# One selective-scan phase: the order of the read-backs, one GpSimd product per half step, and the remainder of the fp32r split made by TensorE

## The chip, the cores and the metric

The kernel runs on one NeuronCore of a Trainium2 chip. The metric is the device time of one execution in microseconds, the median of several runs. TensorE (PE in the profile), VectorE (DVE), ScalarE (ACT), GpSimd (POOL) and SyncE (SP, which here issues every DMA) each run their own instruction list in order and meet only at semaphores.

## The reference

The change lies in the first of two layers. For 8 images of 64 x 64 points with 192 inner channels, four directions k (rows, columns, and both reversed) each make

```
x_dbl = einsum('bkdl,kcd->bkcl', xs, x_proj_w)        # 6 rows for dt, 16 for B, 16 for C
delta = softplus(einsum(x_dbl[:6], dt_proj_w) + dt_proj_b)
h     = exp(delta * A) * h + (delta * u) * B          # 16 states for each channel, along 4096 points
y     = sum over states of h * C, + u * D
```

and the four y are added at their points. The rest (convolution before, normalisation and an output projection after, and a second layer with a Fourier resampling) is not touched.

## The kernel before

The program has three phases, one after another; the middle one, `scan_phase`, is changed. It walks 256 half steps, in the order image b (8), direction k (4), chunk ci of 1024 points (4), half of the channels (2). A half step m has 12 units: group g of four states (4) times block j of 32 channels (3). A unit is one tile of 128 partitions (32 channels x 4 states) by 1024 points. The two half steps of a chunk share the projected B and C. So 128 chunks, and within each an even and an odd half step.

**A unit.** ScalarE makes exp(delta A) (`exp`, line 735). For groups 0 to 2 TensorE spreads B over the partitions into a PSUM pair `P[un % 2]` (`fill`, line 553), VectorE multiplies it by delta u (`multiply`, 640), and scans (`scan`, 660). For group 3 GpSimd makes the product (`multiply`, 795) from a copy `brep`, ScalarE's exponential goes to `P[un % 2]`, and VectorE only scans. GpSimd then multiplies H by the spread C (`weigh`, 803), and TensorE sums the states into `yps` (`sum_y`, 589). Each engine's list is written out by unit number: TensorE does `fill(un + 1)`, ScalarE `exp(un + 1)`, VectorE `multiply(un)` and `scan(un)`, GpSimd `weigh(un - 1)`, and between them at fixed positions x = 0 to 11 of a half step the work for the next chunk. There are 4 buffers H, 3 buffers E (groups 0 to 2) and 7 buffers HC.

**The next chunk's work**, through one PSUM area `stage`, in this order: `project` (TensorE, fp32, line 537, x = 4 and 7 of the even half step, from `u`; for k = 1 and 3 it reads `u` by columns, one element in 64); two copies by ScalarE at x = 8, `dts` (693) and `sx` (694), the latter rounded to fp32r; the remainder `stage - sx` of rows 64 to 95 by VectorE (`split`, 625, after the scan of unit 8), so that the later spread in fp32r adds value and remainder; the delta matmuls (547) at x = 10 and in the odd half step at x = 4; three activations (702 to 706) at x = 11 and 5 that make softplus in `dlu`; VectorE's `delta` (634) that makes `dl`; GpSimd's product `dlu = dl * u` (`delta`, 788), both of them in the odd half step, at x = 1 and x = 7; and the spreads of C and B with their copies (553, 715, 719).

**SyncE** issues in one written order: for each half step the stores of `dl` and `dlu` to DRAM and their return as broadcasts `dlr` and `dur` (`spread_out`, `spread_in`, lines 468 to 485), the store of the finished y (`store_y`, 493), and for k = 2 and 3 the return of the y of the opposite direction into `yp` (`load_y`, 503), which TensorE adds at x = 5 (`sum_y`, line 583). `load_y(n + 1)` stands last in each half step n.

Of the kernel before, what the change touches and what calls it, by code (L numbers as in the profile page):

```python
# [7 lines left out]
ALU = mybir.AluOpType  # L8
# [8 lines left out]
C = 96  # L17
# [287 lines left out]
def scan_phase(nc, ctx, T, S):  # L305
# [13 lines left out]
    ds = T("ds", [C, 2, NK])  # L319
    dsum = T("dsum", [C, 2])  # L320
    idn = T("idn", [C, C])
    dg = T("dg", [C, 2, C])
    dlr = T("dlr", [128, 2 * NJ, TC])
    dur = T("dur", [128, 2 * NJ, TC])
# [30 lines left out]
    u_in = sem("u_in")  # L355
    x_done = sem("x_done")
    sx_copied = sem("sx_copied")
    sx_split = sem("sx_split")
    dt_done = sem("dt_done")
    softplus = sem("softplus_step")  # L360
# [49 lines left out]
    def slot(m, j):  # L410
        return j + NJ * (m % 2)

    def loaded(m):
        return 16 * (m // 2 + 1)
# [16 lines left out]
    def seconds(m):  # L431
        line, rest = divmod(m, NK * 2 * NCH)
        return line * 4 * NCH + max(0, rest - 4 * NCH)

    def rep_index(c, i):
        return 5 * c + i

# [13 lines left out]
    def sync(e):  # L451
        for t, n in consts:
            e.dma_start(t, S[n]).then_inc(consts_in, 16)

        def load_u(b):
            if b:
                e.wait_ge(x_done, 16 * b)
                e.wait_ge(dlu_made, 32 * b)
            for h in range(2):
                e.dma_start(u[:, h, :], S["xa"][b, h]).then_inc(u_in, 16)  # L460

        def spread_out(m):
            if m >= 2:
                for j in range(NJ):
                    e.wait_ge(dlr_in[slot(m, j)], loaded(m - 2))
                    e.wait_ge(dur_in[slot(m, j)], loaded(m - 2))
            e.wait_ge(dl_made, m + 1)
            e.dma_start(S["dl"][m % 2], dl).then_inc(dl_out, 16)
            e.wait_ge(dlu_made, m + 1)
            e.dma_start(S["dlu"][m % 2], dlu[:]).then_inc(dlu_out, 16)  # L470

        def spread_in(m):
            e.wait_ge(dlu_out, 16 * (m + 1))
            for j in range(NJ):
                if m >= 2:
                    e.wait_ge(mul_done, a_index(unit_of(m - 2, GB - 1, j)) + 1)
                    e.wait_ge(pool_mul_done, 3 * (m - 2) + j + 1)
                e.dma_start(dur[:, slot(m, j), :],
                            S["dlu"][m % 2, 32 * j:32 * j + 32, :].unsqueeze(1).to_broadcast([32, 4, TC])).then_inc(
                                dur_in[slot(m, j)], 16)  # L480
            e.wait_ge(dl_out, 16 * (m + 1))
            for j in range(NJ):
                if m >= 2:
                    e.wait_ge(exp_done, unit_of(m - 2, GB, j) + 1)
                e.dma_start(dlr[:, slot(m, j), :],
                            S["dl"][m % 2, 32 * j:32 * j + 32, :].unsqueeze(1).to_broadcast([32, 4, TC])).then_inc(
                                dlr_in[slot(m, j)], 16)

        def store_y(m):
            b, k, ci, half = steps[m]  # L490
            t0 = t_of(k, ci)
            e.wait_ge(y_copied, m + 1)
            e.dma_start(S["yk"][b, k % 2, half, :, t0:t0 + TC], yt[:]).then_inc(y_stored, 16)

        def load_y(m):
            if m == NSTEP or not second(m):
                return
            b, k, ci, half = steps[m]
            t0 = t_of(k, ci)
            e.wait_ge(y_stored, 16 * (steps.index((b, k - 2, NCH - 1 - ci, half)) + 1))  # L500
            if seconds(m):
                e.wait_ge(yp_added, seconds(m))
            e.dma_start(yp[:], S["yk"][b, k % 2, half, :, t0:t0 + TC]).then_inc(yp_in, 16)

        load_u(0)
        for m in range(2):
            spread_out(m)
            spread_in(m)
        for n in range(NSTEP):
            if n % 2 == 0:  # L510
                if n:
                    store_y(n - 1)
                if n + 2 < NSTEP:
                    spread_out(n + 2)
                    spread_in(n + 2)
            else:
                store_y(n - 1)
                if n + 2 < NSTEP:
                    spread_out(n + 2)
                if n % 32 == 29 and n + 3 < NSTEP:  # L520
                    load_u(n // 32 + 1)
                if n + 2 < NSTEP:
                    spread_in(n + 2)
            load_y(n + 1)
        store_y(NSTEP - 1)
        e.wait_ge(y_stored, 16 * NSTEP)

    def tensor(e):
        def project(c, sub):
            b, k, ci, _ = steps[2 * c]  # L530
            t0 = t_of(k, ci) + sub * 512
            if sub == 0:
                if ("x", c) in held:
                    e.wait_ge(*held["x", c])
                e.wait_ge(u_in, 32 * (b + 1))
            for h in range(2):
                r = e.matmul(stage[0:C + NR, sub * 512:(sub + 1) * 512], wx[:, k, h, :], view(k, h, t0, 512),  # L537
                             start=h == 0, stop=h == 1)
            if sub:
                r.then_inc(x_done)  # L540

        def delta(m):
            b, k, ci, half = steps[m]
# [48 lines left out]
                r.then_inc(y_summed)  # L592

        e.wait_ge(consts_in, NCONST)
        e.wait_ge(ve_set, 3)
        project(0, 0)
        project(0, 1)
        delta(0)
        delta(1)
        for i in range(5):  # L600
# [2 lines left out]
        for un in range(NUNIT + 12):  # L603
            n, x = divmod(un, 12)
            c = n // 2 + 1
            fill(un + 1)
            if un >= 5 and (un - 5) % 3 < 2 and (un - 5) // 3 < NG * NSTEP:
                sum_y((un - 5) // 3, (un - 5) % 3)
            if n % 2 == 0:
                if x < 3 and n and n < NSTEP:  # L610
                    rep(c - 1, x + 2)
                if x in (4, 7) and c < NCHUNK:
                    project(c, x // 7)
                if x == 10 and c < NCHUNK:
                    delta(n + 2)
            else:
                if x == 4 and c < NCHUNK:
                    delta(n + 2)
                if x in (8, 10) and c < NCHUNK:
                    rep(c, (x - 8) // 2)  # L620

    def vector(e):
        def split(c):
            e.wait_ge(sx_copied, c + 1)
            e.tensor_tensor(sx[64:96, c % 2, :], stage[64:96, :], sx[64:96, c % 2, :], ALU.subtract).then_inc(sx_split)  # L625

        def delta(m):
            b, k, ci, half = steps[m]
            kk = k * 2 + half
# [34 lines left out]
        e.tensor_copy(selb[:], selbf).then_inc(ve_set)  # L664
        e.memset(c20[:], 20.0).then_inc(ve_set)
        e.tensor_scalar(ndtb[:], dtb[:], -1.0, 20.0, ALU.mult, ALU.add).then_inc(ve_set)
        e.tensor_reduce(dsum[:], ds[:], AX.X, ALU.add).then_inc(skip_made)
        e.wait_ge(skip_made, 1)
        for half in range(2):
            e.tensor_scalar(dg[:, half, :], idn[:], dsum[:, half:half + 1], None, ALU.mult).then_inc(skip_made)  # L670
        split(0)
        delta(0)
        delta(1)
        for un in range(NUNIT):
            n, x = divmod(un, 12)
            c = n // 2 + 1
            if not on_pool(un):
                multiply(un)
            scan(un)
            if c < NCHUNK:  # L680
                if n % 2 == 0 and x == 8:
                    split(c)
                if n % 2 and x == 0:
                    delta(n + 1)
                if n % 2 and x == 6:
                    delta(n + 2)

    def scalar(e):
        def project(c):
            e.wait_ge(x_done, c + 1)  # L690
            if c >= 2:
                e.wait_ge(fill_done, 18 * (c - 1))
            e.copy(dts, stage[C:C + NR, :])
            e.copy(sx[:, c % 2, :], stage[0:C, :]).then_inc(sx_copied)

        def delta(m):
            b, k, ci, half = steps[m]
# [53 lines left out]
        e.activation(am[:], am[:], ACT.Exp).then_inc(a_made)  # L751
        e.wait_ge(a_made, 1)
        e.mul(am[:], am[:], -1.0).then_inc(a_made)
        e.wait_ge(ve_set, 3)
        project(0)
        delta(0)
        delta(1)
        for i in range(5):
# [3 lines left out]
        for un in range(NUNIT + 12):  # L762
# [5 lines left out]
            if n % 2 == 0:  # L768
                if 1 <= x <= 3 and n and n < NSTEP:
                    rep(c - 1, x + 1)  # L770
                if x == 8 and c < NCHUNK:
                    project(c)
                if x == 11 and c < NCHUNK:
                    delta(n + 2)
            else:
                if x == 5 and c < NCHUNK:
                    delta(n + 2)
                if x in (9, 11) and c < NCHUNK:
                    rep(c, (x - 9) // 2)
# [3 lines left out]
    def pool(e):  # L783
# [23 lines left out]
        for un in range(NUNIT + 1):  # L807
# [3 lines left out]
                weigh(un - 1)  # L811
            if n == NSTEP:
                break
            if x in (5, 7, 9):
                multiply(n, (x - 5) // 2)
            if c < NCHUNK and n % 2:
                if x == 1:
                    delta(n + 1)
                if x == 7:
                    delta(n + 2)  # L820

    run_block(nc, sync, tensor, vector, scalar, pool)

# [744 lines left out]
```

## Time and profile before

| | us |
|---|---|
| median of 3 runs (lowest, highest) | 13929.23 (13920.08, 13971.47) |
| the profiled execution: its time | 13937.71 |
| its span in the profile | 13935.9 |
| busy in the span: VectorE, TensorE, GpSimd, ScalarE | 12036.7, 10742.2, 10348.0, 6887.5 |
| mean granted clock of TensorE | 0.742 |

The span is cut by engine into busy and idle time; each idle stretch is put down to the instruction whose semaphore ended it. An instruction's line number names the place in the kernel. A timeline row gives start, duration, engine, line, operation, tiles and count; where neighbouring instructions are alike they are merged into one row with their number, and the bracket holds the engine's idle time before it and who ended it. An fp32 matmul counts as two matmuls in the profile and an fp32r one as one. The scan phase lies between 626 and 11274 us.

### The profile page before, as it was taken

The numbers are of one execution on the slowest core, as the hardware profiler recorded it, in microseconds if no ns is written. First come the engines' busy times: TensorE is split into PE (matmuls) and PEld (weight loads), VectorE is DVE, ScalarE is ACT, GpSimd is POOL, SyncE is SP. The second block draws the span as 40 slices with busy tenths as digits, with TensorE's granted clock in tenths as the row PEclk, the third lists the DMA queues.
The fourth block names the chain that finished last, engine by engine and source line by source line (L and its number), as shares of the span: only waits on it lengthen the run. The fifth ranks groups of instructions, "written<-read, shape, count | busy, mean of one in ns | idle before, by whom it ended". The sixth has DMA issues, their size and how long they took to land. (4 is left out here: it accounts for less than half of the span.)

```text
span 13935.9 us, 133740 instructions
## 1 busy us (share of the span) xinstructions
PE 10742.2 (77%) x41528; PEld 4591.2 (33%) x41528; DVE 12036.7 (86%) x8096; ACT 6887.5 (49%) x9171; POOL 10348.0 (74%) x4494
## 2 busy tenths in 40 slices
PE   8877777777777777777777777777777759999999
PEld 5522222222222222222222222222222237777778
DVE  7699999999999999999999999999999955555554
ACT  4355555555555555555555555555555533444443
POOL 1199889989998998999899999998899962222220
PEclk9866766666666666776677667766666768999999
DMA  3333332333333333333332333333333331111110
GB/s 105 112 102 113 113 122 101 105 118 120 108 105 109 124 108 111 118 104 111 116 121 101 110 115 124 103 103 113 123 111 107 109 90 37 41 40 37 37 37 10
DMA packets 371594, 1357.09 MB, mean 97 GB/s; under 512 B 47080, under 2 KB 47784, under 8 KB 367566
## 3 DMA queue, kind: packets, MB, share of 16 engines
q1 hardware_dynamic: 370894, 1348.53, 29.9%
q8 instruction: 344, 5.64, 0.2%
q14 instruction: 356, 2.92, 0.1%
HBM read 983.45 MB, written 364.90 MB: 97 GB/s over the span
## 5 line engine op out<-in xcount | busy, mean ns | idle before, releaser
L803 POOL TENSOR_TENSOR HC<-H,crep 128x1024 f32<-128x1024 f32 x3072 | 7227.9, 2365 | 989.9 <-DVE H L660 974.2
L553 PE MATMUL psum<-sx,selb 96*128 96x512 f32 x5888 | 3003.7, 610 | 2257.0 <-DVE H L660 1578.4
L660 DVE TENSOR_TENSOR_SCAN H<-E,car,psum 128x1024 f32<-128x1024 f32 x1728 | 4055.6, 2347 | 61.6
L553 PEld LDWEIGHTS psum<-sx,selb 96*128 96x128 f32 x5888 | 1296.9, 268 | 5496.1 <-issue 4553.1
L589 PE MATMUL psum<-HC,sely 128*32 128x512 f32 x12288 | 3080.9, 845 | 12.1 <-POOL HC L803 12.1
L640 DVE TENSOR_TENSOR psum<-dur,psum 128x1024 f32<-128x1024 f32 x2304 | 2784.0, 1208 | 230.4 <-PE psum L553 230.4
L735 ACT ACTIVATE E<-dlr,am 128x1024 f32<-128x1024 f32 x2304 | 2626.5, 1145 | 348.7 <-DVE H L660 347.3
L735 ACT ACTIVATE psum<-dlr,am 128x1024 f32<-128x1024 f32 x768 | 858.6, 1118 | 1971.5 <-DVE H L660 1963.3
L795 POOL TENSOR_TENSOR dbu<-dur,brep 128x1024 f32<-128x1024 f32 x768 | 1814.0, 2362 | 0.0
L741 ACT COPY car<-H 128x1 f32<-128x1 f32 x2304 | 425.7, 185 | 2117.8 <-DVE H L660 2111.1
L660 DVE TENSOR_TENSOR_SCAN H<-psum,car,dbu 128x1024 f32<-128x1024 f32 x576 | 1320.0, 2333 | 96.1 <-POOL dbu L795 93.1
L660 DVE TENSOR_TENSOR_SCAN H<-E,psum 128x1024 f32<-128x1024 f32 x576 | 1317.3, 2287 | 20.0
L547 PE MATMUL psum<-dlt,dtw 6*96 6x512 f32 x1024 | 822.8, 945 | 324.4 <-DVE sx L625 319.6
L1375 ACT ACTIVATE hs<-psum,b1a,co 128x512 f32<-128x512 f32 x768 | 555.7, 778 | 659.0 <-PE psum L41 658.6
L589 PEld LDWEIGHTS psum<-HC,sely 128*32 128x32 f32 x12288 | 376.2, 127 | 1490.1 <-issue 1305.2
L1409 POOL TENSOR_TENSOR y<-y,tmp 96x1024 f32<-96x1024 f32 x64 | 196.8, 3123 | 852.4 <-DMA tmp<-scr_yk 852.4
L537 PE MATMUL psum<-u,wx 96*102 96x512 f32 x1024 | 769.1, 885 | 30.5 <-DMA u<-scr_xa 30.5
L1155 PE MATMUL psum<-w2s,hs 128*128 128x96 f32 x6144 | 770.6, 284 | 0.6 <-DVE hs L1292 0.6
L788 POOL TENSOR_TENSOR dlu<-dlt,u 96x1024 f32<-96x1024 f32 x256 | 667.6, 2608 | 136.5 <-DVE dlt L634 136.5
L1155 PEld LDWEIGHTS psum<-w2s,hs 128*128 128x128 f32 x6144 | 731.6, 197 | 33.1 <-issue 5.3
L1292 DVE SCALAR_TENSOR_TENSOR hs<-psum,b1p,hs 128x512 f32<-128x512 f32 x768 | 544.2, 748 | 180.6 <-ACT hs L1375 180.4
L41 PE MATMUL psum<-xu,w1s 128*128 128x512 f32 x2304 | 603.1, 406 | 2.2 <-DVE xu L1279 2.2
(127 smaller groups left out, 10005.9 us busy)
## 6 DMA issues: line engine op xcount, KB each, us to landing
dur<-scr_dlu SPq DMA_DIRECT2D x768, 512.0 KB, 4.5
dlr<-scr_dl SPq DMA_DIRECT2D x768, 512.0 KB, 7.1
scr_dl<-dlt SPq DMA_DIRECT2D x256, 384.0 KB, 3.0
scr_dlu<-dlu SPq DMA_DIRECT2D x256, 384.0 KB, 3.0
scr_yk<-yt SPq DMA_DIRECT2D x256, 384.0 KB, 3.4
yp<-scr_yk SPq DMA_DIRECT2D x128, 384.0 KB, 8.9
scr_xa<-xs SPq DMA_DIRECT2D x64, 384.0 KB, 3.5
scr_sz<-xs SPq DMA_DIRECT2D x64, 384.0 KB, 3.5
```

Source lines behind the costliest of these rows:

```text
L41: r = e.matmul(o, w[p], x[q], start=first and i == 0, stop=last and i == 2)
L537: r = e.matmul(stage[0:C + NR, sub * 512:(sub + 1) * 512], wx[:, k, h, :], view(k, h, t0, 512), start=h == 0, stop=h == 1)
L547: r = e.matmul(stage[0:C, sub * 512:(sub + 1) * 512], dtw[C:C + NR, k * ND + half * C:k * ND + (half + 1) * C], dts[:, sub * 512:(sub + 1) ...
L553: r = e.matmul(o[:, sub * 512:(sub + 1) * 512], selb[:, which, :], sx[:, c % 2, sub * 512:(sub + 1) * 512], start=True, stop=True)
L589: r = e.matmul(yps[32 * j:32 * j + 32, cols], sely[:], HC[:, (3 * i + j) % NHC, cols], start=g == 0 and k == 1, stop=g == NG - 1)
L640: e.tensor_tensor(P[un % 2], dur[:, slot(m, j), :], P[un % 2], ALU.mult).then_inc(mul_done)
L660: e.tensor_tensor_scan(H[:, un % NH, ::step], decay[:, ::step], drive[:, ::step], init, ALU.mult, ALU.add).then_inc(scan_done)
L735: e.activation(o, dlr[:, slot(m, j), :], ACT.Exp, scale=am[:, ae:ae + 1]).then_inc(exp_done)
L788: e.tensor_tensor(shaped(dlu[:], k), shaped(dl, k), view(k, half, t_of(k, ci), TC), ALU.mult).then_inc(dlu_made)
L795: e.tensor_tensor(dbu[:, j, :], dur[:, slot(m, j), :], brep[:], ALU.mult).then_inc(pool_mul_done)
L803: e.tensor_tensor(HC[:, un % NHC, :], H[:, un % NH, :], crep[:, g, :], ALU.mult).then_inc(hc_done)
L1155: r = e.matmul(o[:, i * C:(i + 1) * C], hs[:, q % 2, j, i * 128:(i + 1) * 128], w2s[:, j, :], start=j == 0, stop=j == 2)
```

## The change

Three edits are made together.

1. SyncE's order: the stores and returns are split into four functions and regrouped. In an even half step n the `dlu` of n + 1 goes out and comes back, then y is stored and `load_y(n + 1)` follows. In an odd one `dl` and `dlu` of n + 1 go out and in, y is stored, `load_y(n + 1)` follows, and only then does SyncE wait for the `dl` of n + 2.
2. GpSimd makes `dlu` once in each half step, at x = 1 (`delta(n + 1)`; at the last half step of an image still one half step ahead, at x = 7), and its products for group 3 at x = 3, 5, 7 in place of 5, 7, 9.
3. The remainder: VectorE's `split` is gone. TensorE's new `rest(c)`, at x = 9 of the even half step, waits for the copy `sx`, repeats the projection into `stage` (fp32) and adds minus `sx` to it by a matmul in fp32r with `nid` (minus the identity, zero in rows 0 to 63). ScalarE's new `split(c)`, at x = 9 too, waits for that and copies rows 64 to 95 into `sx`. The delta matmuls wait for this copy, as they did for VectorE's.

```diff
         for n in range(NSTEP):
             if n % 2 == 0:
                 if n:
+                    if not ends_image(n + 1):
+                        out_dlu(n + 1)
+                        in_dur(n + 1)
                     store_y(n - 1)
+                load_y(n + 1)
+            else:
+                if n + 1 < NSTEP:
+                    out_dl(n + 1)
+                    out_dlu(n + 1)
+                    in_dur(n + 1)
+                    in_dlr(n + 1)
+                store_y(n - 1)
+                load_y(n + 1)
                 if n + 2 < NSTEP:
-                    spread_out(n + 2)
-                    spread_in(n + 2)
-            else:
-                store_y(n - 1)
-                if n + 2 < NSTEP:
-                    spread_out(n + 2)
-                if n % 32 == 29 and n + 3 < NSTEP:
-                    load_u(n // 32 + 1)
-                if n + 2 < NSTEP:
-                    spread_in(n + 2)
-            load_y(n + 1)
+                    out_dl(n + 2)
+                    if ends_image(n + 2):
+                        out_dlu(n + 2)
+                        if n + 3 < NSTEP:
+                            load_u(n // 32 + 1)
+                        in_dur(n + 2)
+                    in_dlr(n + 2)
...
+        def rest(c):
+            b, k, ci, _ = steps[2 * c]
+            t0 = t_of(k, ci)
+            e.wait_ge(sx_copied, c + 1)
+            for sub in range(2):
+                cols = slice(sub * 512, (sub + 1) * 512)
+                for h in range(2):
+                    e.matmul(stage[0:C, cols], wx[:, k, h, 0:C], view(k, h, t0 + sub * 512, 512), start=h == 0, stop=False)
+                r = e.matmul(stage[0:C, cols], nid[:], sx[:, c % 2, cols], start=False, stop=True)
+            r.then_inc(rest_done)
...
+                if x == 9 and c < NCHUNK:
+                    rest(c)
                 if x == 10 and c < NCHUNK:
                     delta(n + 2)
...
-                if n % 2 == 0 and x == 8:
-                    split(c)
...
+        def split(c):
+            e.wait_ge(rest_done, c + 1)
+            e.copy(sx[64:96, c % 2, :], stage[64:96, :]).then_inc(sx_split)
...
                 if x == 8 and c < NCHUNK:
                     project(c)
+                if x == 9 and c < NCHUNK:
+                    split(c)
                 if x == 11 and c < NCHUNK:
                     delta(n + 2)
...
-            if x in (5, 7, 9):
-                multiply(n, (x - 5) // 2)
-            if c < NCHUNK and n % 2:
-                if x == 1:
-                    delta(n + 1)
-                if x == 7:
-                    delta(n + 2)
+            if x == 1 and 2 <= n + 1 < NSTEP and not ends_image(n + 1):
+                delta(n + 1)
+            if x in (3, 5, 7):
+                multiply(n, (x - 3) // 2)
+            if x == 7 and n + 2 < NSTEP and ends_image(n + 2):
+                delta(n + 2)
```

## Rows read from the trace of the kernel before

**Rows 1.** Busy time of each engine over 10 ms of the scan phase (windows).

```profile
core 0: us, PE busy (x) PEld busy (x) DVE busy (x) ACT busy (x) POOL busy (x), PEclk, DMA share, GB/s
1000.00:11000.00 10000.00, 7348.71 (x19768) 2118.72 (x19769) 9580.05 (x5430) 5258.49 (x6880) 9076.49 (x3860) 0.69 0.33 112
```

**Rows 2.** The page's costliest groups: busy, mean ns, idle before with its releaser.

```profile
L803 POOL TENSOR_TENSOR HC<-H,crep 128x1024 f32<-128x1024 f32 x3072 | 7227.9, 2365 | 989.9 <-DVE H L660 974.2
...
L640 DVE TENSOR_TENSOR psum<-dur,psum 128x1024 f32<-128x1024 f32 x2304 | 2784.0, 1208 | 230.4 <-PE psum L553 230.4
...
L795 POOL TENSOR_TENSOR dbu<-dur,brep 128x1024 f32<-128x1024 f32 x768 | 1814.0, 2362 | 0.0
```

**Rows 3.** Who waited for GpSimd's products, line 795 (total us, times).

```profile
  DVE H L660: 131.1, 129
```

**Rows 4.** Timeline of VectorE at the end of an even half step.

```profile
5416.78 2.35 DVE L660 TENSOR_TENSOR_SCAN H<-E,car,psum 128x1024 f32<-128x1024 f32 x1
5419.16 1.22 DVE L625 TENSOR_TENSOR sx<-psum,sx 32x1024 fp32r<-32x1024 f32 x1
5420.41 6.83 DVE L660 TENSOR_TENSOR_SCAN H<-psum,car,dbu 128x1024 f32<-128x1024 f32 x3
5427.16 1.21 DVE L640 TENSOR_TENSOR psum<-dur,psum 128x1024 f32<-128x1024 f32 x1
```

**Rows 5.** Timeline of GpSimd near the end of an odd half step.

```profile
5046.17 2.84 POOL L788 TENSOR_TENSOR dlu<-dlt,u 96x1024 f32<-96x1024 f32 x1
...
5053.60 2.36 POOL L795 TENSOR_TENSOR dbu<-dur,brep 128x1024 f32<-128x1024 f32 x1
```

**Rows 6.** Timeline of VectorE in the same odd half step.

```profile
5055.99 2.29 DVE L660 TENSOR_TENSOR_SCAN H<-psum,dbu 128x1024 f32<-128x1024 f32 x1 [2.20 <-POOL dbu L795]
```

**Rows 7.** Timeline of SyncE's queue around a read-back of y.

```profile
5348.35 0.30 SPq L468 DMA_DIRECT2D scr_dl<-dlt  x1
...
5359.40 0.69 SPq L503 DMA_DIRECT2D yp<-scr_yk  x1
```

**Rows 8.** Timeline of TensorE at the use of that y.

```profile
5368.47 1.99 PE L583 MATMUL psum<-yp,idn 96*96 96x512 f32 x2 [3.71 <-DMA yp<-scr_yk]
...
5372.24 1.22 PE L553 MATMUL psum<-sx,selb 96*128 96x512 f32 x2
```

**Rows 9.** Timeline of VectorE at the same place.

```profile
5373.51 1.23 DVE L640 TENSOR_TENSOR psum<-dur,psum 128x1024 f32<-128x1024 f32 x1 [3.39 <-PE psum L553]
```

**Rows 10.** Timeline of ScalarE in the even half step of rows 4.

```profile
5416.97 1.00 ACT L693 COPY dlt<-psum 6x1024 f32<-6x1024 f32 x1
5417.98 1.01 ACT L694 CAST sx<-psum 96x1024 fp32r<-96x1024 f32 x1
5419.22 1.12 ACT L735 ACTIVATE psum<-dlr,am 128x1024 f32<-128x1024 f32 x1 [0.23 <-DVE H L660]
...
5422.85 1.12 ACT L735 ACTIVATE psum<-dlr,am 128x1024 f32<-128x1024 f32 x1 [2.40 <-DVE H L660]
```

**Rows 11.** Timeline of TensorE in that half step; the next chunk has k = 2.

```profile
5412.26 0.70 PE L553 MATMUL psum<-sx,selb 96*128 96x512 f32 x2 [0.95 <-DVE H L660]
5412.80 1.88 PE L537 MATMUL psum<-u,wx 96*102 96x512 f32 x4
5414.60 1.92 PE L589 MATMUL psum<-HC,sely 128*32 128x512 f32 x12
5420.43 3.72 PE L547 MATMUL psum<-dlt,dtw 6*96 6x512 f32 x4 [3.91 <-DVE sx L625]
```

**Rows 12.** Timeline of TensorE in another; the next chunk has k = 3.

```profile
2929.86 3.59 PE L537 MATMUL psum<-u,wx 96*102 96x512 f32 x4
2933.38 1.92 PE L589 MATMUL psum<-HC,sely 128*32 128x512 f32 x12
2937.49 1.95 PE L547 MATMUL psum<-dlt,dtw 6*96 6x512 f32 x4 [2.20 <-DVE sx L625]
2942.21 1.19 PE L553 MATMUL psum<-sx,selb 96*128 96x512 f32 x2 [2.76 <-DVE H L660]
```

**Rows 13.** Windows over the matmuls at 2929.86, 5412.80 and 5420.43; the clock is third from last.

```profile
2929.90:2933.40 3.50, 3.50 (x8) 0.52 (x6) 3.46 (x3) 0.63 (x1) 3.50 (x2) 1.00 0.00 0
5412.80:5414.70 1.90, 1.90 (x8) 0.60 (x9) 1.86 (x2) 0.00 (x0) 1.90 (x2) 1.00 0.03 9
5420.40:5424.20 3.80, 3.72 (x4) 0.95 (x4) 3.79 (x2) 1.40 (x4) 3.80 (x3) 0.50 0.00 0
```

More of the change, by code:

```diff
@@ L321, in scan_phase @@
     idn = T("idn", [C, C])
+    nid = T("nid", [C, C], F32R)
     dg = T("dg", [C, 2, C])
@@ L357, in scan_phase @@
     sx_copied = sem("sx_copied")
+    rest_done = sem("rest_done")
     sx_split = sem("sx_split")
@@ L433, in seconds, with ends_image @@
         return line * 4 * NCH + max(0, rest - 4 * NCH)
+    def ends_image(m):
+        return m % (NK * 2 * NCH) == NK * 2 * NCH - 1
     def rep_index(c, i):
@@ L460, in load_u, with out_dl @@
                 e.dma_start(u[:, h, :], S["xa"][b, h]).then_inc(u_in, 16)
-        def spread_out(m):
+        def out_dl(m):
             if m >= 2:
@@ L465, in spread_out, with out_dlu, in_dur @@
                     e.wait_ge(dlr_in[slot(m, j)], loaded(m - 2))
-                    e.wait_ge(dur_in[slot(m, j)], loaded(m - 2))
             e.wait_ge(dl_made, m + 1)
             e.dma_start(S["dl"][m % 2], dl).then_inc(dl_out, 16)
+        def out_dlu(m):
+            if m >= 2:
+                for j in range(NJ):
+                    e.wait_ge(dur_in[slot(m, j)], loaded(m - 2))
             e.wait_ge(dlu_made, m + 1)
             e.dma_start(S["dlu"][m % 2], dlu[:]).then_inc(dlu_out, 16)
-        def spread_in(m):
+        def in_dur(m):
             e.wait_ge(dlu_out, 16 * (m + 1))
@@ L480, in spread_in, with in_dlr @@
                                 dur_in[slot(m, j)], 16)
+        def in_dlr(m):
             e.wait_ge(dl_out, 16 * (m + 1))
@@ L506, in sync @@
         for m in range(2):
-            spread_out(m)
-            spread_in(m)
+            out_dl(m)
+            out_dlu(m)
+            in_dur(m)
+            in_dlr(m)
         for n in range(NSTEP):
@@ L594, in tensor @@
         e.wait_ge(consts_in, NCONST)
-        e.wait_ge(ve_set, 3)
+        e.wait_ge(ve_set, 4)
         project(0, 0)
         project(0, 1)
+        rest(0)
         delta(0)
@@ L622, in vector @@
     def vector(e):
-        def split(c):
-            e.wait_ge(sx_copied, c + 1)
-            e.tensor_tensor(sx[64:96, c % 2, :], stage[64:96, :], sx[64:96, c % 2, :], ALU.subtract).then_inc(sx_split)
         def delta(m):
@@ L666, in vector @@
         e.tensor_scalar(ndtb[:], dtb[:], -1.0, 20.0, ALU.mult, ALU.add).then_inc(ve_set)
+        e.tensor_scalar(nid[:, 0:64], idn[:, 0:64], 0.0, None, ALU.mult)
+        e.tensor_scalar(nid[:, 64:96], idn[:, 64:96], -1.0, None, ALU.mult).then_inc(ve_set)
         e.tensor_reduce(dsum[:], ds[:], AX.X, ALU.add).then_inc(skip_made)
@@ L670, in vector @@
             e.tensor_scalar(dg[:, half, :], idn[:], dsum[:, half:half + 1], None, ALU.mult).then_inc(skip_made)
-        split(0)
         delta(0)
@@ L753, in scalar @@
         e.mul(am[:], am[:], -1.0).then_inc(a_made)
-        e.wait_ge(ve_set, 3)
+        e.wait_ge(ve_set, 4)
         project(0)
+        split(0)
         delta(0)
```

## The prediction

> **What bounds the kernel now.** I read the busy time in windows first. Over 10 ms of the scan phase VectorE is busy 9580 of 10000 us, GpSimd 9076, TensorE 7349 and ScalarE 5258 [rows 1]: VectorE sets the pace, and only what leaves its list or ends a wait of its own is worth time. Next I read what VectorE waits for. Its products wait 230.4 us for TensorE's fills [rows 2], its scans 131.1 us in 129 places for GpSimd's products [rows 3]. The timelines then show both places.
>
> The wait for GpSimd sits at unit 11 of the odd half step: 2.20 us [rows 6]. GpSimd had made a `dlu` (2.84 us) at x = 7 and came to its third product only at 5053.60, when the scan could have begun [rows 5, 6].
>
> The wait for TensorE sits in odd half steps with k = 2 and 3. `load_y` was issued at 5359.40, behind the return of a `dl` that was stored only at 5348.35, in the same half step [rows 7]. TensorE waited 3.71 us for it with a fill queued behind; that fill ended at 5373.46, and VectorE had waited 3.39 us [rows 8, 9]. There are 64 such half steps, and 64 x 3.4 is 218, nearly all of the 230.
>
> **What the change takes away.** (1) VectorE's remainder. From the scan of unit 8 to the next scan is 5420.41 - 5416.78 = 3.63 us; without it the distance would be that of the other scans, (5427.16 - 5420.41) / 3 = 2.25. It costs 1.37 us (the scan's own start-to-start is slightly over 2.25), 128 times: 175 us [rows 4]. (2) The wait for `yp`. `load_y` no longer stands behind a `dl` that VectorE has yet to make. What is now ahead of it (the `dlu` made at x = 1, its return, the store of y at x = 4) is done before `yp` is free at x = 6, so it is issued at about 22 us of a half step, some 16 us before the one begins that needs it. I give it its whole 230 us. (3) GpSimd's products. A half step costs it 12 x 2.365 + 3 x 2.362 + 2.84 = 38.3 us, now evenly [rows 2, 5]. VectorE's shortest is 9 x (1.21 + 2.35), less about 0.5 of overlap, and 3 x 2.25, also 38.3, and odd ones are some 2.4 longer for two `delta`. The third product follows the weighing of unit 6, some 6 us ahead of its scan. GpSimd stays within its four buffers and the 131 us go. Sum of the gains: 175 + 230 + 131 = 536 us, or 4.2 us for each chunk.
>
> The other moved DMAs cost nothing: the first scan ends 3.6 us into a half step (1.21 + 2.35), so `dlu` is made at about 3.6 + 2.4 + 2.8 = 9 us, and its broadcasts are due when the half step is over, at 38. Two set-up instructions on VectorE are below 1 us.
>
> **What the change adds.** `rest` is four fp32 matmuls and two fp32r ones, each of 512 columns. `project` does two such fp32 ones in 1.88 us where the next chunk's k is 0 or 2 [rows 11], but in 3.59 us where it is 1 or 3, at a granted clock of 1.00 in both [rows 12, 13]; there it reads `u` one element in 64. The fp32r matmul is half of a fill, 0.35 us, or 0.6 at the low clock [rows 11, 12]. So `rest` takes 2 x (1.88 + 0.35) = 4.5 us, or 2 x (3.59 + 0.35) = 7.9 us, half of the chunks each.
>
> TensorE has room for this. But the work is a chain, `sx` copied, `rest`, `split`, delta, and what counts is what stands behind its waits. On ScalarE, `split` stands at x = 9, ahead of `exp` of unit 11 at x = 10. That exponential cannot overtake it, and unit 11 cannot be scanned without it.
>
> In the even half step of [rows 4, 10] the copy ends at 5418.99. Then: `rest` 5419.04 to 5423.50 at the full clock; `split` 1.01 us as the copies of 6 and of 96 partitions (the nearest rows, same length), to 5424.56; `exp` 1.12 us, to 5425.71. Without the remainder VectorE's scans would start at 5419.04, 5421.30 and 5423.55. The last waits until 5425.75: 2.2 us. At the low clock `rest` is 2 x (3.75 + 0.6) = 8.7 and the wait 6.4.
>
> Which clock? TensorE ended at 5416.52, so it would be idle for 2.5 us before `rest`. After 2.20 us the delta matmuls ran at 1.95 us, the full clock [rows 12], after 3.91 us at 3.72, clock 0.50 [rows 11, 13]. I take the nearer row for most and a microsecond for the others: a wait of 3.2 us.
>
> For k = 1 and 3 the copy ends at the same place, and `rest` is 3.4 us longer: 2.2 + 3.4 = 5.6. TensorE's sums ahead of it start later, after the longer `project` (2933.38), and at the low clock they would end about 1 us after the copy; I add 0.3: 5.9 us. Both ends: 5.6, and 7.1 with that microsecond and 2 x 0.25 for fp32r at the low clock.
>
> Next in line: the delta matmuls (1.95 or 3.72) and then the fill of unit 12 (0.70 or 1.19) follow `split` on TensorE. VectorE wants that fill 1.2 + 2.25 = 3.45 us after `split` ends. At the full clock it is there after 2.75, hidden; at the low one after 5.0, 1.55 late. I take half of that for k = 1 and 3 (0.8) and 0.15 for the others.
>
> Loss: 64 x (5.9 + 0.8) = 429 and 63 x (3.2 + 0.15) = 211, together 640 us. The first chunk's is before the loop.
>
> **Weighed against the skill.** The Trainium skill (FP8 and Floating Point Precision, TensorE Precision Notes) says that true fp32 takes four passes through the array. From that I estimate 4 x 512 columns at 2.4 GHz as 0.85 us a matmul, whatever the reading pattern. The rows agree for k = 0 and 2 (0.94) and not for k = 1 and 3 (1.80). The same skill (Advanced Engine Details and Errata, SBUF Cachelines) says that accesses which each fall on another 16-byte line are penalised, which sides with the slow row. By the four passes alone the change would save 257 us (as rival C), by the rows it costs 104; the measured rows decide.
>
> **Sum.** +640 - 536 = +104 us on the profiled execution's 13937.7. That one was 8.5 us over the median of its kernel, so a median of about 14033.
>
> **The rivals.**
> A, as forecast, 4.6 to 6.0 us a chunk against the 4.2 gained: 13980 to 14160.
> B, the clock stays full everywhere and nothing is late behind `split`: 64 x 5.6 + 63 x 2.2 = 497, so -39, and about 13890; up to 13980. For it: a gap of 2.5 is near the 2.20.
> C, faster: `rest` runs at the fp32 rate of contiguous reading for every k. The mechanism is the matmul's read of `u`; if the 3.59 us had another cause (such as the writes of 102 rows, which `rest` cuts to 96), the wait is 2.2 everywhere: 127 x 2.2 = 279 and -257, 13672. It decides below a mean wait of 4.2. Against it: the same 102 rows take 1.88 in [rows 11].
> D, TensorE sinks to the low clock at this place each time: 63 x (6.4 + 1.55) + 64 x (7.1 + 1.55) = 1054, so +518, 14447. For it: mean granted clock 0.69 [rows 1] and clock 0.50 at the delta matmuls of [rows 13]. Against: more work, closer together. A half-way case ends near 14250.
> E, `load_y` stays late for a reason that I miss (then the gain is only 306): +334, 14263.
>
> **Chances.** A 0.50, B 0.20, C 0.12, D 0.13, E 0.05. A difference of 0.5%, some 70 us, is about what a measurement of this kernel can tell from no change. Faster by more: C, 0.12. Within: B and the lower part of A, 0.30. Slower: 0.58. For the range, C and the far part of D are left out: 13880 to 14210; A alone 13980 to 14160.
>
> **What the new profile should show.** Line 625 is gone, and VectorE's wait for line 795 and TensorE's for `yp` are near zero. VectorE's scans of unit 11 in even half steps wait for ScalarE's exponential, 2 to 4 us for k = 0 and 2 ahead, 5.5 to 7 for k = 1 and 3, some 600 us in 127 places. ScalarE's new copy waits for TensorE. I am wrong if ScalarE's exponential of unit 11 starts before the copy's end or is not what VectorE waits for, if `rest` takes under 5 us for k = 1 and 3, or if GpSimd or `yp` still holds VectorE.

## The result, and the profile after

The changed kernel is slower: a median of 14085.07 us (14050.13 to 14143.42, 8 runs) against 13956.6 us (13920.08 to 14047.23, 8 runs) for the kernel before on the same chips. The ratio is 1.0093 with a 95% interval of 1.0070 to 1.0115. The forecast was +104 us on the kernel before; measured are +128 us by the medians.

VectorE, which bounds the scan phase, is less busy after (9316 us where [rows 1] have 9580), and still the phase is longer. The same window after:

```profile
core 0: us, PE busy (x) PEld busy (x) DVE busy (x) ACT busy (x) POOL busy (x), PEclk, DMA share, GB/s
1000.00:11000.00 10000.00, 7864.98 (x20736) 2278.99 (x20736) 9316.01 (x5248) 5312.08 (x6930) 8962.12 (x3818) 0.72 0.34 111
```

So VectorE waits more, by some 260 us in this window. The page's groups after (they answer to [rows 2]), with one more, the scans of group 3:

```profile
L671 DVE TENSOR_TENSOR psum<-dur,psum 128x1024 f32<-128x1024 f32 x2304 | 2785.3, 1209 | 100.4 <-PE psum L585 99.8
...
L832 POOL TENSOR_TENSOR dbu<-dur,brep 128x1024 f32<-128x1024 f32 x768 | 1818.3, 2368 | 0.0
...
L691 DVE TENSOR_TENSOR_SCAN H<-psum,car,dbu 128x1024 f32<-128x1024 f32 x576 | 1317.7, 2330 | 406.9 <-issue 394.1
```

The two old waits are gone: no scan waits for line 832 any more, where [rows 3] had 131.1 us in 129 places, and 88 of the 99.8 us for fills are, as shown below, at another place than [rows 8, 9]. The other 11.5 us are a single wait before the first product of the phase, which every kernel of this study has. They are in the 230.4 us of [rows 2] too, so that the read-back of y was worth 219 us and not 230. New is the idle time before the scans of group 3. The list of VectorE's waits in the window gives all of it (us in total, times, longest):

```profile
DVE H L691 <- issue: 513.1, 117, 7.2
DVE psum L671 <- PE psum L585: 81.6, 77, 1.6
DVE H L691 <- ACT psum L769: 12.6, 2, 6.3
```

"Issue" means that the profile names no releaser. The timelines name it. First VectorE, ScalarE and TensorE at the end of an even half step whose next chunk has k = 2 (they answer to [rows 4, 10, 11]):

```profile
5316.70 4.57 DVE L691 TENSOR_TENSOR_SCAN H<-psum,car,dbu 128x1024 f32<-128x1024 f32 x2
5323.69 2.35 DVE L691 TENSOR_TENSOR_SCAN H<-psum,car,dbu 128x1024 f32<-128x1024 f32 x1 [2.42 <-issue]
```

```profile
5315.53 1.01 ACT L724 CAST sx<-psum 96x1024 fp32r<-96x1024 f32 x1
5316.88 1.12 ACT L769 ACTIVATE psum<-dlr,am 128x1024 f32<-128x1024 f32 x1 [0.34 <-DVE H L691]
5321.58 1.00 ACT L728 CAST sx<-psum 32x1024 fp32r<-32x1024 f32 x1 [3.58 <-PE psum L571]
5322.49 1.10 ACT L769 ACTIVATE psum<-dlr,am 128x1024 f32<-128x1024 f32 x1
```

```profile
5313.74 3.64 PE L621 MATMUL psum<-HC,sely 128*32 128x512 f32 x12
5317.30 2.06 PE L570 MATMUL psum<-u,wx 96*96 96x512 f32 x4
5318.80 0.80 PE L571 MATMUL psum<-sx,nid 96*96 96x512 f32 x1
5319.44 1.88 PE L570 MATMUL psum<-u,wx 96*96 96x512 f32 x4
5320.76 0.79 PE L571 MATMUL psum<-sx,nid 96*96 96x512 f32 x1
5322.64 2.04 PE L579 MATMUL psum<-dlt,dtw 6*96 6x512 f32 x4 [1.09 <-ACT sx L728]
5324.60 1.22 PE L585 MATMUL psum<-sx,selb 96*128 96x512 f32 x2
```

The scan of unit 11 could have started at 5321.27, when the two before it were over. It starts at 5323.69, 0.1 us after ScalarE's exponential (5322.49 + 1.10), which follows the copy of the remainder (5321.58), which follows `rest` (lines 570 and 571, 5317.30 to 5321.55). That is the chain of the prediction, link by link. It holds in all 127 even half steps that have a `rest`: the exponential starts as the copy ends, and the scan 0.09 us after the exponential's end. One thing is not typical here: `rest` began 0.76 us after `sx` was copied, behind TensorE's sums (5313.74, at a granted clock of 0.50). In 58 of the 63 half steps of this kind TensorE had instead stood idle for 2.2 to 2.5 us, as forecast.

Then the same place where the next chunk has k = 3 (VectorE, ScalarE, TensorE; they answer to [rows 12]):

```profile
5653.80 2.35 DVE L691 TENSOR_TENSOR_SCAN H<-psum,car,dbu 128x1024 f32<-128x1024 f32 x1 [5.02 <-issue]
5657.66 1.23 DVE L671 TENSOR_TENSOR psum<-dur,psum 128x1024 f32<-128x1024 f32 x1 [1.51 <-PE psum L585]
```

```profile
5651.70 1.00 ACT L728 CAST sx<-psum 32x1024 fp32r<-32x1024 f32 x1 [6.19 <-PE psum L571]
```

```profile
5644.11 3.65 PE L570 MATMUL psum<-u,wx 96*96 96x512 f32 x4 [0.70 <-ACT sx L724]
...
5647.83 3.59 PE L570 MATMUL psum<-u,wx 96*96 96x512 f32 x4
5650.43 1.23 PE L571 MATMUL psum<-sx,nid 96*96 96x512 f32 x1
5652.75 3.72 PE L579 MATMUL psum<-dlt,dtw 6*96 6x512 f32 x4 [1.09 <-ACT sx L728]
5656.40 1.22 PE L585 MATMUL psum<-sx,selb 96*128 96x512 f32 x2
```

`rest` takes 7.55 us (5644.11 to 5651.66), VectorE waits 5.02 us. Here the second wait shows too: the delta matmuls run at 3.72 us, and VectorE waits another 1.51 us for the fill behind them. The clock in windows over the two projections and over the delta matmuls (third from last):

```profile
5644.10:5647.80 3.70, 3.69 (x5) 0.96 (x6) 3.70 (x3) 1.12 (x1) 3.70 (x3) 1.00 0.00 0
5647.80:5651.40 3.60, 3.60 (x6) 0.70 (x4) 0.98 (x1) 0.00 (x0) 3.59 (x2) 1.00 0.00 0
5652.80:5656.40 3.60, 3.60 (x4) 0.90 (x4) 2.35 (x1) 2.06 (x2) 0.17 (x1) 0.50 0.00 0
```

The times of the profiled executions say less than their scan phases. This one took 14143.42 us, the slowest of its 8. Its last scans, of this form, and those of the kernel before (first and last start in us):

```profile
L691 DVE TENSOR_TENSOR_SCAN H<-psum,car,dbu x576: 2323/2326/2352, 780.4 to 11395.7; 128x1024 f32<-128x1024 f32 x192
```

```profile
L660 DVE TENSOR_TENSOR_SCAN H<-psum,car,dbu x576: 2323/2326/2353, 780.6 to 11269.2; 128x1024 f32<-128x1024 f32 x192
```

The scan phase grew by 11395.7 - 11269.2 = 126.5 us. The other 79 us of the difference of spans (14141.6 - 13935.9 = 205.7) lie in the third phase, which no kernel of this study touches. It took between 2638 and 2744 us in the eleven traces, so below the ends of the scan phases are compared beside the times.

### The profile page after: what moved, and what is told of

Read it like the earlier page. It is cut to its first block and busy times, and to the rows that moved or that the text cites. A ratio compares the mean times of both kernels' runs of the same rounds, so it can differ in the third digit from the quotient of the medians.

```text
span 14141.6 us, 136556 instructions
## 1 busy us (share of the span) xinstructions
PE 11466.1 (81%) x42808; PEld 4838.1 (34%) x42808; DVE 11871.6 (84%) x7970; ACT 7009.1 (50%) x9299; POOL 10336.8 (73%) x4494
## 5 line engine op out<-in xcount | busy, mean ns | idle before, releaser
L585 PE MATMUL psum<-sx,selb 96*128 96x512 f32 x5888 | 2921.4, 594 | 1997.6 <-DVE H L691 1207.9
L621 PE MATMUL psum<-HC,sely 128*32 128x512 f32 x12288 | 2996.2, 823 | 9.8 <-POOL HC L840 9.8
L585 PEld LDWEIGHTS psum<-sx,selb 96*128 96x128 f32 x5888 | 1244.6, 258 | 5139.7 <-issue 4091.3
L671 DVE TENSOR_TENSOR psum<-dur,psum 128x1024 f32<-128x1024 f32 x2304 | 2785.3, 1209 | 100.4 <-PE psum L585 99.8
L570 PE MATMUL psum<-u,wx 96*96 96x512 f32 x1024 | 796.7, 913 | 170.2 <-ACT sx L724 170.2
```

The source lines that it names most:

```text
L570: e.matmul(stage[0:C, cols], wx[:, k, h, 0:C], view(k, h, t0 + sub * 512, 512), start=h == 0, stop=False)
L585: r = e.matmul(o[:, sub * 512:(sub + 1) * 512], selb[:, which, :], sx[:, c % 2, sub * 512:(sub + 1) * 512], start=True, stop=True)
L621: r = e.matmul(yps[32 * j:32 * j + 32, cols], sely[:], HC[:, (3 * i + j) % NHC, cols], start=g == 0 and k == 1, stop=g == NG - 1)
L671: e.tensor_tensor(P[un % 2], dur[:, slot(m, j), :], P[un % 2], ALU.mult).then_inc(mul_done)
```

## The experiments

All idle stretches ahead of VectorE's instructions were sorted by unit and by k of the next chunk. The sums are in us, with the number of places. Left out are stretches under 0.06 us, the 11.5 us before the first product, and the fills of unit 8 in the even half step (at most 34 us, in rest_fit2). "Old waits" are those for the read-back of y and for GpSimd's products:

| kernel | unit 11, even, k 0/2 | unit 11, even, k 1/3 | fills of the first units, odd | old waits, odd | last scan starts |
|---|---|---|---|---|---|
| before | 0 | 0 | 0 | 219 + 131 | 11269.2 |
| changed | 203 (63) | 358 (64) | 89 (85) | 0 | 11395.7 |
| order_only | 0 | 0 | 0 | 0 | 10900.4 |
| order_only2 | 0 | 0 | 0 | 0 | 10896.0 |
| rest_only | 205 (63) | 347 (64) | 88 (92) | 227 + 131 | 11765.8 |
| exp_first | 0 | 0 | 653 (127) | 0 | 11387.1 |
| no_rest | 0 | 0 | 39 (64) | 0 | 10761.0 |
| flat_rest | 205 (63) | 130 (64) | 42 (65) | 0 | 11119.4 |
| rest_fit | 0 | 0 | 140 (78) | 0 | 10892.0 |
| rest_fit2 | 0 | 0 | 106 (76) | 0 | 10871.2 |
| rest_fit3 | 0 | 0 | 23 (42) | 0 | 10770.1 |

**order_only**: the two reorderings without the third edit.

```diff
-                if x == 9 and c < NCHUNK:
-                    rest(c)
...
+                if n % 2 == 0 and x == 8:
+                    split(c)
...
-                if x == 9 and c < NCHUNK:
-                    split(c)
```

> Edits 1 and 2 alone (SyncE's order, GpSimd's places); VectorE keeps the remainder. Theory (the chain behind TensorE's remainder is the whole loss, the two waits the rest of the gain): the waits for the read-back and for GpSimd's products go, 230 + 131 us, and nothing is added: 13957 - 361 = about 13600, ratio 0.974. Rival (the new order by itself brings waits, by later dlu or fuller queues): less than half of that, 13800 or more.

Measured: 13564.12 us, ratio 0.9709 (0.9662 to 0.9757). Both old waits are gone and none came. The last scan starts 368.8 us earlier, where 230 + 131 = 361 were expected. The waits that went are 219 + 131 = 350 us. The rest is in VectorE's busy time, which falls by 21 us (10161 to 10140 between the first and the last scan) although its instructions last as long in sum as before (10410 and 10407): what no longer waits overlaps the instruction before it. The rival falls. Edits 1 and 2 were not tried apart; that each took away its own wait is read from the two waits. Run again beside rest_fit3 as order_only2:

> order_only once more, beside rest_fit3 on one chip: edits 1 and 2 with the remainder on VectorE. Both theories: 13560, ratio 0.971. It is the mark for whether moving the remainder to TensorE is worth anything: 175 us of VectorE's work less what waits remain.

Measured: 13576.42 us, ratio 0.9727 (0.9706 to 0.9747).

**rest_only**: the third edit in the old order of SyncE and GpSimd.

```diff
+                if x == 9 and c < NCHUNK:
+                    rest(c)
...
-                if n % 2 == 0 and x == 8:
-                    split(c)
...
+                if x == 9 and c < NCHUNK:
+                    split(c)
```

> Edit 3 alone (the remainder on TensorE) in the old order. Theory: +650 us of waits at unit 11 and at the next fill, -175 us of VectorE's work, and the old waits of 361 us stay: 13957 + 475 = about 14430, ratio 1.034. Rival (the new wait hides the old ones, since GpSimd catches up while VectorE waits): the waits for GpSimd's products go too and it is 14300.

Measured: 14491.84 us, ratio 1.0365 (1.0325 to 1.0404). VectorE's waits in the 1000 to 11000 us window:

```profile
DVE H L672 <- issue: 496.9, 115, 6.3
DVE psum L652 <- PE psum L566: 282.0, 139, 5.4
DVE H L672 <- POOL dbu L813: 122.4, 116, 2.2
```

The old wait for GpSimd (line 813 here) stands in full beside the new ones, so the rival falls; the last scan starts 496.6 us later, where 475 were expected. Gain and loss don't hide each other: the parts are +496.6 us (rest_only) and -368.8 (order_only) by the last scan, together +127.8, and the whole change is +126.5.

**exp_first**: ScalarE's copy behind the exponential of unit 11.

```diff
-                if x == 9 and c < NCHUNK:
+                if x == 10 and c < NCHUNK:
                     split(c)
```

> The changed kernel with ScalarE's copy of the remainder behind the exponential of unit 11 (x = 10 for x = 9), nothing else. Theory (the chain also holds the fill of unit 12 on TensorE, behind the delta matmuls): the wait at unit 11 goes, a wait for the fill of unit 12 takes its place, 5.2 to 6.8 us where the next k is 1 or 3 and 2.5 to 4.5 where it is 0 or 2: about 14000 to 14100, at most 100 us below the changed kernel. Rival (only ScalarE's order counts): all 650 us go, 13430.

Measured: 14059.7 us, ratio 1.0074 (1.0047 to 1.0101). VectorE and TensorE at the end of an even half step, k = 1 next:

```profile
5144.22 6.81 DVE L691 TENSOR_TENSOR_SCAN H<-psum,car,dbu 128x1024 f32<-128x1024 f32 x3
5157.56 1.23 DVE L671 TENSOR_TENSOR psum<-dur,psum 128x1024 f32<-128x1024 f32 x1 [6.53 <-PE psum L585]
```

```profile
5153.57 2.80 PE L579 MATMUL psum<-dlt,dtw 6*96 6x512 f32 x4 [1.09 <-ACT sx L728]
5156.30 1.22 PE L585 MATMUL psum<-sx,selb 96*128 96x512 f32 x2
```

The three scans of group 3 now run without a gap, and the whole wait stands one unit later, at the fill behind the delta matmuls. ScalarE's order was the first thing that the chain blocked; TensorE's order is the second, worth as much, hidden behind it. One move alone gives back 8.6 us of scan phase.

**no_rest**: leaves out the repeated projection; `rest` is one fp32r matmul over half of the columns. All waits stay.

```diff
             for sub in range(2):
                 cols = slice(sub * 512, (sub + 1) * 512)
-                for h in range(2):
-                    e.matmul(stage[0:C, cols], wx[:, k, h, 0:C], view(k, h, t0 + sub * 512, 512), start=h == 0, stop=False)
-                r = e.matmul(stage[0:C, cols], nid[:], sx[:, c % 2, cols], start=False, stop=True)
+                if sub:
+                    r = e.matmul(stage[0:C, cols], nid[:], sx[:, c % 2, cols], start=True, stop=True)
```

> The changed kernel without the repeated projection: rest is one fp32r matmul of 0.35 us in place of four fp32 and two fp32r ones; every wait and place is kept (the remainder is not computed). Theory (the loss is the length of rest within the chain): no wait at unit 11 nor at the next fill, about 13430. Rival (the handovers TensorE to ScalarE and back, or the copy, make part of it): above 13550.

Measured: 13481.35 us, ratio 0.9667 (0.9619 to 0.9716). No wait at unit 11 is left. 39 us remain at the next fill, so that "no wait at the next fill" was wrong by 0.6 us in half of the chunks. The last scan starts 508.2 us earlier than before; the prediction's gain of 536 us less those 39 is 497. The time is 51 us over the expectation: 39 of it are these waits, the rest is not assigned.

**flat_rest**: `rest` reads `u` by rows for every k, so that for k = 1 and 3 the remainder is of other points.

```diff
-wx[:, k, h, 0:C], view(k, h, t0 + sub * 512, 512), start=h == 0, stop=False)
+wx[:, k, h, 0:C], u[:, h, t0 + sub * 512:t0 + sub * 512 + 512], start=h == 0, stop=False)
```

> The changed kernel with rest reading u by rows for every k, with the same number of matmuls, columns and waits (for k = 1 and 3 the remainder is of other points, so the result is not the reference's). Theory (reading u one element in 64 is what makes rest 3.4 us longer there): rest takes 4.5 to 6 us for every k, the waits of the 64 half steps fall from 5.6 + 1.1 to about 3.2 + 0.3 us, -205 us against the changed kernel: about 13880, ratio to before 0.994. Rival (the 3.59 us have another cause than the reading pattern): no change from 14085.

Measured: 13831.88 us, ratio 0.9894 (0.9857 to 0.9931). The number of matmuls, rows and columns is unchanged, and the wait at unit 11 for k = 1 and 3 falls from 358 / 64 = 5.6 us to 130 / 64 = 2.0. `rest` itself takes 4.14 us on average there, in place of 7.65. The pattern in which `u` is read is the cause of the longer `rest`. The last scan starts 276 us earlier than in the changed kernel. I had expected a wait of 3.2 us, as for k = 0 and 2. Those stay at 205 / 63 = 3.25 because of the clock: TensorE stands idle for 2.2 us on average before `rest`, which then takes 4.13 to 8.00 us, over 5 us in 43 of 63 half steps. For k = 1 and 3 it is still at its sums, after a longer `project`: it is idle for 0.3 us on average and never over 1.01, and `rest` takes 4.13 to 4.15 us in all 64.

**rest_fit**: the chain moved, all else as changed.

```diff
+            if n % 2 == 0 and x == 11 and c < NCHUNK:
+                delta(n + 2)
...
-                if x in (4, 7) and c < NCHUNK:
-                    project(c, x // 7)
-                if x == 9 and c < NCHUNK:
+                if x in (4, 6) and c < NCHUNK:
+                    project(c, x // 6)
+                if x == 8 and c < NCHUNK:
                     rest(c)
-                if x == 10 and c < NCHUNK:
-                    delta(n + 2)
```

ScalarE's `project` is at x = 7 and copies `sx` before `dts`, its `split` at x = 10; softplus, `dl` and `dlu` of the even half step's delta are at x = 0, 1 and 2 of the odd one.

> The changed kernel with the chain made to fit: the projection at x = 4 and 6, its copies at x = 7 with sx first, rest at x = 8, the copy of the remainder behind the exponential of unit 11, the even half step's delta matmuls behind the fill of unit 12, and softplus, dl and dlu of the even half step each one unit later. Theory: none of these is late, VectorE waits under 1 us a chunk: 13957 - 536 = about 13430, ratio 0.962. Rival (TensorE's load itself is too much at the lower clock, so that fills come late wherever it is put): above 13600.

Measured: 13553.36 us, ratio 0.9703 (0.966 to 0.9745). That is 123 us over the expectation, and below the rival's 13600: the theory missed a wait. Both waits of the changed kernel are gone, but a new one of 2.1 us stands before the product of unit 13 in 61 odd half steps, where the next k is 0 or 2. TensorE and VectorE there:

```profile
5261.43 1.12 PE L585 MATMUL psum<-sx,selb 96*128 96x512 f32 x2 [3.94 <-ACT sx L728]
5262.48 3.73 PE L579 MATMUL psum<-dlt,dtw 6*96 6x512 f32 x4
5266.14 1.93 PE L621 MATMUL psum<-HC,sely 128*32 128x512 f32 x6
5267.99 1.22 PE L585 MATMUL psum<-sx,selb 96*128 96x512 f32 x2
```

```profile
5269.26 1.23 DVE L671 TENSOR_TENSOR psum<-dur,psum 128x1024 f32<-128x1024 f32 x1 [2.22 <-PE psum L585]
```

TensorE was idle for 3.94 us, then the delta matmuls took 3.73 us, and two fills stood around them.

**rest_fit2**: the delta matmuls behind the fill of unit 13.

```diff
-            if n % 2 == 0 and x == 11 and c < NCHUNK:
-                delta(n + 2)
+            if n % 2 and x == 0 and c < NCHUNK:
+                delta(n + 1)
```

Softplus, `dl` and `dlu` follow at x = 1, 2 and 3.

> As rest_fit, with the even half step's delta matmuls behind the fill of unit 13 instead of unit 12, and softplus, dl and dlu of that half step one unit later again. rest_fit's own trace has VectorE waiting 2.1 us, 61 times, for the fill of unit 13, which stood behind delta matmuls at the low clock. Theory: that wait goes, -130 us against rest_fit: about 13430, ratio 0.961. Rival (the low clock makes something else late instead): as rest_fit, 13550.

Measured: 13554.9 us, ratio 0.9705 (0.9672 to 0.9739). A miss: the wait moved on to the fill of unit 14 (97 us in 61 places). Putting slow work one fill later only made the next fill late.

**rest_fit3**: where the next k is 0 or 2, copy and delta matmuls earlier instead.

```diff
+                if x == 10 and c < NCHUNK and steps[n + 2][1] % 2 == 0:
+                    delta(n + 2)
...
-            if n % 2 == 0 and x == 11 and c < NCHUNK:
+            if n % 2 == 0 and x == 11 and c < NCHUNK and steps[n + 2][1] % 2:
...
-                if x == 10 and c < NCHUNK:
+                if c < NCHUNK and x == 9 + steps[n + 2][1] % 2:
                     split(c)
```

> As rest_fit where the next chunk has k = 1 or 3; where it has k = 0 or 2, the copy of the remainder at x = 9 and the delta matmuls at x = 10, ahead of the fill of unit 12 (rest is over at 31.3 us of the half step there and TensorE then stood idle until 36.3, after which it ran at the low clock). Theory (the idle stretch brings the low clock and with it the late fill): the delta matmuls start after some 2 us of idleness, run at the full clock, VectorE's 131 us of waits in 64 chunks go: 13553 - 130 = about 13425, and some 130 us below order_only2. Rival (TensorE's added load costs the same wherever it stands, as rest_fit and rest_fit2 suggest with 13553 and 13555): 13550, equal to order_only2.

Measured: 13492.34 us, ratio 0.9659 (0.9636 to 0.9682), beside order_only2's 0.9727 on the same chip: 84 us faster than it, and 3.4% faster than the kernel before. By the last scans, of one profiled execution each, it is 126 us ahead of order_only2 and 122 ahead of rest_fit, where 130 were expected. TensorE in the same half step:

```profile
5197.33 3.66 PE L579 MATMUL psum<-dlt,dtw 6*96 6x512 f32 x4 [1.82 <-ACT sx L730]
5200.91 1.22 PE L585 MATMUL psum<-sx,selb 96*128 96x512 f32 x2
```

The expected reason held in part. The delta matmuls ran at the full clock (under 2.2 us) in 33 of the 63 half steps, where 2 did in rest_fit, but in 17 they took over 3.3 us still (58 in rest_fit), as in this one, after 1.82 us of idleness. What helps in all of them is the place: they begin in TensorE's idle stretch, before the fill of unit 12 and not behind it. In the 17 slow ones that fill is 0.14 to 0.58 us late, in the other 46 VectorE waits for no fill of units 12 to 14. With 23 us of waits left at the first fills, TensorE's added load is not what cost the time.

## Why the prediction was right

The direction, the place and the chain held. Of the terms, the small one of the next fill (5) was sized too small, and the wait for k = 0 and 2 (4) came out right by luck.

1. **VectorE's remainder, 175 us.** The even half steps, from last scan to last scan, take 39.54 us on average before and in order_only, and 38.10 in no_rest: 1.44 us, forecast 1.37.
2. **The read-back of y and GpSimd's products, 361 us.** The waits that went are 219 + 131 = 350 us; the prediction had taken the 11.5 us before the first product for a part of the read-back. order_only's scan phase is 369 us shorter.
3. **The wait at unit 11, k = 1 and 3 next.** 358 / 64 = 5.60 us, forecast 5.9. `rest` takes 7.65 us on average, not 7.9: in the profile its fp32r matmuls overlap with the next fp32 ones. The sums at the low clock are there as forecast: `rest` starts 0.30 us after the copy on average, and 1.39 at most.
4. **The same, k = 0 and 2 next.** 203 / 63 = 3.22 us, forecast 3.2, but its two parts were both off. At the full clock `rest` takes 4.14 us, not 4.5, and the wait is then 1.8 us on average, not 2.2. And the full clock was there in only 23 of the 63 half steps, not in most: in 25 `rest` took 5.8 us and VectorE waited 3.3 to 3.6, in 15 it took 7.3 to 7.5 and VectorE waited 4.9 to 5.3. The clock cost some 1.4 us on average where 1.0 was put down. "The nearer row" was no guide to it, as the last section shows; that the errors cancel is luck.
5. **The fill behind the delta matmuls.** 18 us for k = 0 and 2 (forecast 63 x 0.15 = 9) and 70 us for k = 1 and 3 (forecast 64 x 0.8 = 51). This term was sized too small: delta matmuls after a long `rest` took the low clock's 3.7 us more often than half of the time (37 of 64 over 3.3 us, 7 below 2.2). VectorE waits in 56 places for 1.25 us each.

Loss 650 us, forecast 640; gain, 127 x 1.44 + 350 = 533, forecast 536. The difference is 117, and the scan phase grew by 126.5; the last 10 us are not assigned. The third phase alone differs by up to 106 us between the profiled executions, so that the times, +104 forecast and +128 measured, prove less here than the terms do.

Of the rivals, B (497 us of waits) and D (1054) are excluded by the 650, E by order_only. C is refuted twice. `rest` took 3.65 and 3.59 us a half at 5644.11 and 5647.83. And in flat_rest, with the same 96 rows read side by side, `rest` takes 4.14 us and the scan phase is 276 us shorter (253 by the medians, 14085 - 13832), so the reading pattern is the cause of the 3.59 us. The forecast had taken the slow row. The Trainium skill (Advanced Engine Details and Errata, SBUF Cachelines) names such a penalty for accesses that each fall on another line. flat_rest agrees, with 2.0 us of wait in place of 5.6, but no run here varied the step.

## What to carry to other kernels

Work taken from the engine that sets the pace is paid back where its replacement is a chain through other engines' in-order lists: look at what stands behind each new wait on each engine, and when that is due, not at how idle the engine is (ScalarE and TensorE had room here, 53% and 73% busy). Such a chain blocks several lists at once, so moving one item shows almost no gain (exp_first) until all are moved (rest_fit). A slow item of it did no good one fill later (rest_fit2), and did good in an idle stretch before the fill (rest_fit3). Measure edits of one change apart: two of these three together gave 2.7 to 2.9%, and the third took 3.7%. Well placed, the third is worth having: rest_fit3 is 0.6% faster than order_only2.

## What was not expected of the hardware

The clock after an idle stretch is not told by the length of that stretch. Three half steps of the changed kernel, all with k = 2 next, have `rest` behind almost the same idleness:

```profile
5397.68 1.99 PE L570 MATMUL psum<-u,wx 96*96 96x512 f32 x4 [2.46 <-ACT sx L724]
5479.34 1.96 PE L570 MATMUL psum<-u,wx 96*96 96x512 f32 x4 [2.52 <-ACT sx L724]
5560.10 3.73 PE L570 MATMUL psum<-u,wx 96*96 96x512 f32 x4 [2.52 <-ACT sx L724]
```

The granted clock was 1.00, 1.00 and 0.99 in the 4 us before. Over the three `rest` it was (third from last):

```profile
5397.70:5403.40 5.70, 5.70 (x10) 2.11 (x10) 4.36 (x2) 1.23 (x2) 5.70 (x4) 0.70 0.00 0
5479.40:5483.40 4.00, 4.00 (x10) 1.49 (x10) 4.00 (x3) 1.23 (x2) 3.98 (x3) 1.00 0.00 0
5560.20:5567.40 7.20, 7.20 (x10) 2.49 (x10) 4.46 (x2) 1.23 (x2) 7.00 (x4) 0.55 0.00 0
```

The first `rest` lost the full clock on its way, the second never did, the third ran at the low one from its start. The delta matmuls say the same. They ran at 1.95 us after 2.20 us of idleness in [rows 12], at 3.66 after 1.82 us in rest_fit3, and at 3.72, clock 0.50, after only 1.09 us in the changed kernel at 5652.75, behind 7.5 us of matmuls at a granted clock of 1.00. What decides between them stays open.

For these strided fp32 reads the clock hardly matters here. Of the fp32 matmuls that read one element in 64, four records (two matmuls) took 3.59 us at the full clock ([rows 12, 13]). In the kernel before, this is one such group with the window over it, at the low one:

```profile
1842.37 3.62 PE L537 MATMUL psum<-u,wx 96*102 96x512 f32 x4
1842.40:1846.00 3.60, 3.60 (x6) 1.31 (x5) 3.53 (x3) 2.25 (x4) 2.48 (x2) 0.50 0.37 109
```

In that trace's `project` they took 3.59 to 3.60 us in 59 groups of four at the full clock and 3.61 to 3.62 in 35 at the low one. The same groups with `u` read side by side took 1.88 us (86) and 3.61 to 3.62 (22).
